# Turning the rotated heads of two units in one run of TensorE transposes, in every second unit

## The chip, the cores and the metric

The kernel runs on one core of one Trainium2 chip. The metric is the device time of one execution in microseconds (us); lower is better. The engines are called by the profile's names: PE is TensorE's matmul, PEld its weight load, DVE is VectorE, ACT ScalarE, POOL GpSimd, and SP is SyncE, which here issues nearly all DMAs.

## What is computed

The reference takes `x` (32 sequences of 32 tokens, 512 wide), adds a small per-sequence linear layer to it, and then adds an attention layer with paged keys and values:

```
x = x + einsum('bct,bcd->bdt', x, weights[subjects])
q = rope(rmsnorm(x @ Wq.T))        # 32 heads of 128
k = rope(rmsnorm(x @ Wk.T))        # 8 heads of 128
v = x @ Wv.T                       # 8 heads of 128
k_all = concat(k_cache[block_table], k)   # 512 old keys, masked by length, and 32 new ones
v_all = concat(v_cache[block_table], v)
x = x + (softmax(q k_all^T * SCALE) v_all) @ Wo.T
```

The normalised heads are rotated in halves: `t1*cos - t2*sin` and `t2*cos + t1*sin`.

## The kernel before

The kernel has two phases in one program. The first one makes queries, keys and values and writes them to DRAM. The second one computes scores, softmax, the weighted sum and the output projection for 256 pairs of a sequence and a key head. Precision is kept by splitting numbers in a high and a low half, so most products are three matmuls.

**The units of the first phase.** The 1024 tokens are 8 tiles of 128 (`g`). The columns of the weights are 12 chunks of 512 (`c`): 8 of Wq, 2 of Wk, 2 of Wv. A unit `u` is one chunk with one tile of tokens, and there are NU = 96 units in the order chunk by chunk: units 0 to 63 make queries, 64 to 79 keys, 80 to 95 values. The first NN = 80 are normalised and rotated. Each engine runs its own loop over the units, and semaphores tie the loops together.

**What becomes of a rotated unit.** PE makes 12 matmuls into one of three PSUM banks (`ps_proj`, line 1533). ACT takes the squares of the four heads (L1114). DVE multiplies the bank with the cosine and sine tables into `rot` (L1397 for queries, four instructions L1405 for keys) and signals `v_proj`. POOL adds the two products of each half into `roped`, one of NRP = 3 buffers (L909), and signals `p_sum`. Three units later (LAG = 3), PE transposes the four heads of 128x128 into one of two banks `ps_rt` (L1709) and signals `t_rt`. ACT rounds that bank to the high half in a buffer `stage` (L1127, `a_rthi`), DVE forms the low half (L1415, `v_rtlo`), and one unit later SP stores the `stage` buffer, one of NST = 8, to `q_t` or `k_new_t` in DRAM (L751). Key units also need `rstd` from POOL (L931, L933) ahead of the rotation.

**The waits around it.** In its loop PE may start unit `u` when DVE has rotated unit `u` - 3 (three banks `ps_proj`). It may transpose unit `un` when POOL has added it, and when DVE has formed the low half of unit `un` - 2, which held the same bank. POOL may write `roped` for unit `u` when unit `u` - 3 has been transposed. ACT may write `stage` for `un` when the store of `un` - 8 has landed.

**The other work in the same loops.** Each unit also carries a task on the caches and weights (`TASKS`): a 512 KB piece of a cache or of Wo is loaded into one of four buffers `c_nat` (L684), and either scanned for its largest values (ACT L1139 or DVE L1425) or converted, that is split into halves (`c_stage`, ACT L1147 and DVE L1429) and stored again (L761, L764). The load for task t + 4 is issued by SP when task t is done. The next chunk of weights is split by ACT (`wt_hi`, L1014 or L1017) and DVE (`wt_lo`, L1229 or L1233), and in the first chunk the tokens themselves are transposed and split on the way (`x0t_hi` L1021, `x0t_lo` L1223). SP also loads pages of keys into `kt`, one a unit, from unit 54 for the first sequence and from unit 80 (`NEXT_KEYS_AT`) for the second; the second one's buffer lies where the first phase's `rot` and `roped` lie.

SP takes its loop strictly in order: for unit `u` first the load of weights, then the store of turned heads, then the tasks of the unit, then pages.

Of the kernel before, what the change touches and what calls it, by code (L numbers as in the profile page):

```python
# [59 lines left out]
def build(nc, x, rows_in, table, l0_w, wq_t, wk_t, wv_t, wo_t, norms_in, kc_t, v_cache, wv,  # L60
# [186 lines left out]
    t_proj, a_proj, v_proj = sem("t_proj"), sem("a_proj"), sem("v_proj")  # L247
# [33 lines left out]
    NN = NG * (HK + NHALF)  # L281
    LAG = 3
    NCONV = 2 * NKCH

    PAGES_AT, XSUM_AT, K_TABLE_AT = 13, 15, 49
    XSUM_BOUND = float(np.sqrt(HID)) * (1.0 + 2.0**-10)
# [354 lines left out]
    def all_stored(eng):  # L641

        for i in range(NST):
            eng.wait_ge(d_st[i], 16 * (NU // NST))
        converted(eng, NCONV)

    def converted(eng, n):

        for i in range(NCS):
            eng.wait_ge(d_cst[i], 16 * len(range(i, n, NCS)))  # L650

    with persist, nc.Block() as block:
        @block.sync
        def _(sp):
# [82 lines left out]
            for u in range(NU):  # L737
                c, g = units[u]
                if u == NG:
                    sp.wait_ge(v_x0, NG)  # L740
                    sp.dma_start(x0_d.rearrange("g p h -> p g h"), x0[:]).then_inc(d_x0, 16)
                if g == 0 and c + 2 < NCK:
                    load_w(c + 2)
                if LAG < u <= NN + LAG:
                    un = u - LAG - 1
                    cn, gn = units[un]
                    kind, _, k = chunks[cn]
                    sp.wait_ge(v_rtlo, un + 1)
                    at_k = k if kind == "q" else NHALF - 1 - k
                    dst = (q_t if kind == "q" else k_new_t)[GB * gn:GB * (gn + 1), :, at_k * BLK:(at_k + 1) * BLK]  # L750
                    sp.dma_start(dst.rearrange("b d f -> d b f"), stage[un % NST][:].rearrange("p (b f) -> p b f", b=GB)  # L751
                                 ).then_inc(d_st[un % NST], 16)
                for t in TASK_IN[u]:
                    kind, n = TASKS[t]
                    if kind == "scan":
                        scanned(sp, n)
                    else:
                        what, ch = conv_kind(n)
                        sp.wait_ge(v_clo, n + 1)
                        if what == "k":  # L760
                            sp.dma_start(k_pages_t[GB * ch:GB * (ch + 1)].rearrange("a d f -> d a f"),  # L761
                                         c_stage[n % NCS][:].rearrange("p (a f) -> p a f", a=GB)).then_inc(d_cst[n % NCS], 16)
                        else:
                            sp.dma_start(v_pages[P * ch:P * (ch + 1)], c_stage[n % NCS][:]).then_inc(d_cst[n % NCS], 16)  # L764
                    if t + NCN < len(TASKS):
                        load_c(t + NCN)
                if u == NN + 3:
                    sp.wait_ge(v_scaled, 1)
                    for a in range(GB):
                        sp.dma_start(rows_d.rearrange("(q t) a c g -> a t q (c g)", t=SEQ)[a],  # L770
                                     row_part[SEQ * a:SEQ * (a + 1)].rearrange("p j c g -> p j (c g)")).then_inc(d_rows, 16)
                if u == NN + 7:
                    sp.wait_ge(d_rows, 16 * GB)
                    sp.dma_start(row_scale[:], rows_d).then_inc(d_rowl, 16)
                if u == KEYS_AT:
                    converted(sp, NKCH)
                    sp.wait_ge(v_rope, 4)
                    sp.wait_ge(v_vrow, 1)
                if KEYS_AT <= u < KEYS_AT + NPP:
                    load_pages(0, u - KEYS_AT, 1)  # L780
                if u == PREFETCH:
                    for i in range(NST):
                        sp.wait_ge(d_st[i], 16 * len(range(i, NN, NST)))
                    load_queries(0)
                    load_queries(1)
                if u == NEXT_KEYS_AT:
                    converted(sp, NCONV)
                if NEXT_KEYS_AT <= u < NEXT_KEYS_AT + NPP:
                    load_pages(1, u - NEXT_KEYS_AT, 1)
                if u in WO_LOADS:  # L790
                    wo_scanned(sp)
                    sp.wait_ge(t_rt, NN)
                    sp.wait_ge(v_wlo, HPC * (NCK - 1) if WO_LOADS[u] == 0 else HPC * NCK)
                    if WO_LOADS[u] >= 2:
                        sp.wait_ge(t_proj, NU - NG)
                    load_wo(WO_LOADS[u])
                if u == NEW_V_AT:
                    sp.wait_ge(d_st[(NU - NG) % NST], 16 * ((NU - NG) // NST + 1))
                    load_new_v(0)
                if u > NN:  # L800
                    un = u - 1
                    cn, gn = units[un]
                    sp.wait_ge(v_proj, un + 1)
                    k = HPC * chunks[cn][2]
                    sp.dma_start(v_new[GB * gn:GB * (gn + 1), :, :, k:k + HPC].rearrange("b t s j d -> (b t) s (j d)"),
                                 stage[un % NST][:].rearrange("p (s f) -> p s f", s=2)).then_inc(d_st[un % NST], 16)
            un = NU - 1
# [51 lines left out]
        def _(pool):  # L859
# [88 lines left out]

            converted(pool, NCONV)
            pool.wait_ge(v_vrow, 1)  # L950
# [50 lines left out]
        def _(act):  # L1001
# [96 lines left out]
            for u in range(NU):  # L1098
# [20 lines left out]
                else:  # L1119
                    act.wait_ge(d_st[u % NST], 16 * (u // NST))  # L1120
                    act.activation(v_staged(u, 0), ps_proj[u % NPJ][:].rearrange("p (j d) -> p j d", j=HPC),
                                   ACT.Copy, scale=scale[:, VS:VS + 1]).then_inc(a_proj, 1)
                if LAG <= u < NN + LAG:
                    un = u - LAG
                    act.wait_ge(t_rt, un + 1)
                    act.wait_ge(d_st[un % NST], 16 * (un // NST))
                    act.activation(staged(un)[:, :, 0], turned(un), ACT.Copy).then_inc(a_rthi, 1)  # L1127
# [52 lines left out]
        def _(dve):  # L1180
# [188 lines left out]
            for u in range(NU):  # L1369
# [38 lines left out]
                else:  # L1408
                    dve.scalar_tensor_tensor(v_staged(u, 1), ps_proj[u % NPJ][:].rearrange("p (j d) -> p j d", j=HPC),
                                             scale[:, VS:VS + 1], v_staged(u, 0), ALU.mult, ALU.subtract  # L1410
                                             ).then_inc(v_proj, 1)
                if LAG <= u < NN + LAG:
                    un = u - LAG
                    dve.wait_ge(a_rthi, un + 1)
                    dve.tensor_tensor(staged(un)[:, :, 1], turned(un), staged(un)[:, :, 0], ALU.subtract  # L1415
                                      ).then_inc(v_rtlo, 1)
# [113 lines left out]
        def _(pe):  # L1530
# [141 lines left out]
            for u in range(NU):  # L1672
# [25 lines left out]
                    scores(u - SCORES_AT)  # L1698
                if c == 0 and g + 2 < NG:
                    l0(g + 2)  # L1700
                if LAG <= u < NN + LAG:
                    un = u - LAG
                    pe.wait_ge(p_sum, un + 1)
                    if un == 1:
                        pe.wait_ge(v_wsum, 2)
                    if un >= 2:
                        pe.wait_ge(v_rtlo, un - 1)
                    for j in range(HPC):
                        last = pe.transpose(turned_head(un, j), roped[un % NRP][:, j, :], ident[:])  # L1709
                    last.then_inc(t_rt, 1)  # L1710
# [89 lines left out]
```

## Time and profile before

| | |
|---|---|
| median of 3 runs | 998.41 us (996.98 to 1000.1) |
| the profiled execution | 997.23 us, of which its span from first to last instruction is 995.4 us |
| first phase (PE's 96 units) | to about 346 us |
| PE busy over the span | 96% |
| DVE, ACT, POOL busy | 83%, 76%, 58% |
| TensorE's granted clock | 0.998 of full speed |

All durations used below come from the one profiled execution. Busy shares are averages over two very different phases, so they don't say which engine sets the pace in a given stretch. A matmul's duration includes its way through the array and overlaps the next one's; how fast matmuls follow each other is seen from start to start.

### The profile page before, as it was taken

The page shows a single profiled execution, that of the slowest core. Times are in us where ns is not written, and L with a number is a line of the kernel's source. Part 1 is how long each engine was busy: PE and PEld are TensorE (multiplying, and loading weights), DVE is VectorE, ACT ScalarE, POOL GpSimd, SP SyncE. Part 2 cuts the span into 40 slices and gives each one's busy share as a digit, 9 for nine tenths or more (in the row PEclk, how much of TensorE's full clock was granted, in tenths as well). Part 3 has the DMA queues.
Part 4 walks back from the last instruction along what each step waited for, and adds up shares of the span by engine and source line. Part 5 has one row for each costly group of instructions (what it writes and reads, how often), then busy time and mean ns, then how long its engine had stood idle before and what let it go on. Part 6 is the DMA issues. An engine that isn't in the chain of part 4 may idle for free.

```text
span 995.4 us, 25120 instructions
## 1 busy us (share of the span) xinstructions
PE 958.1 (96%) x8075; PEld 796.9 (80%) x8075; DVE 827.7 (83%) x1842; ACT 761.0 (76%) x2108; POOL 579.3 (58%) x861
## 2 busy tenths in 40 slices
PE   5899999999899999899999999999999999989998
PEld 4578888888677788788888888888888888878885
DVE  7889999999997689888878878888887887877880
ACT  5898999988884688878777778777777877767760
POOL 5565665565893067667755655565565656655550
PEclk9999999999999999999999999999999999999999
DMA  5899999989998899999999999999999999999940
GB/s 196 301 319 330 323 381 374 381 279 390 397 341 283 327 321 364 339 280 286 294 317 266 284 327 272 286 305 275 321 273 283 332 258 280 331 286 242 271 126 11
DMA packets 249907, 294.92 MB, mean 296 GB/s; under 512 B 79024, under 2 KB 206512, under 8 KB 247216
## 3 DMA queue, kind: packets, MB, share of 16 engines
q1 hardware_dynamic: 231088, 226.07, 76.6%
q0 software_dynamic: 18688, 67.25, 18.0%
q8 instruction: 65, 1.06, 0.4%
q14 instruction: 66, 0.54, 0.2%
HBM read 231.77 MB, written 46.27 MB: 279 GB/s over the span
## 4 chain that ended last, share of the span: by engine, by line
PE 75%; DVE 10%; POOL 5%; issue 5%; ACT 2%; DMA 2%; SPq 0%; DVEq 0%; ACTq 0%; POOLq 0%
PE ps_proj L1533 17%; PE ps_y L1533 16%; PE ps_o L1614 14%; PE ps_s L1571 8%; PE ps_t L1585 7%; PE ps_s L1575 7%; PE ps_rt L1709 2%; DMA c_nat<-in_L_cond_v_cache 2%; POOL vs L944 1%; DVE c_stage L1429 1%; DVE probs L1267 1%; DVE rot L1405 1%; PE ps_o L1626 1%; DVE stage L1415 1%; POOL probs L963 1%
## 5 line engine op out<-in xcount | busy, mean ns | idle before, releaser
L1039 ACT ACTIVATE probs<-probs,neg_max 128x544 f32<-128x544 f32 x256 | 191.6, 748 | 115.4 <-DVE neg_max L1267 100.2
L1267 DVE CUSTOM_DVE_ANT_0 probs<-ps_s,mask,row_scale 128x544 f32<-128x544 f32 x256 | 200.4, 783 | 53.7 <-PE ps_s L1575 43.3
L1614 PE MATMUL ps_o<-pt,vs 128*128 128x128 f16 x3072 | 214.0, 220 | 1.1 <-DMA vs<-v_pages,v_row 1.0
L1614 PEld LDWEIGHTS ps_o<-pt,vs 128*128 128x128 f16 x3072 | 193.1, 98 | 16.2 <-DMA vs<-v_pages,v_row 2.0
L963 POOL TENSOR_SCALAR probs<-probs,recip 128x512 f32<-128x512 f32 x144 | 99.8, 693 | 168.6 <-DVE recip L1275 164.6
L909 POOL TENSOR_TENSOR roped<-rot 128x256 f32<-128x256 f32 x160 | 144.1, 921 | 80.2 <-DVE rot L1397 76.1
L1533 PE MATMUL ps_proj<-wt_hi,x0t_hi 128*128 128x512 f32 x384 | 158.6, 414 | 6.2 <-DVE x0t_lo L1223 5.8
L1287 DVE SCALAR_TENSOR_TENSOR pt<-ps_t,pt 128x512 f16<-128x512 f32 x190 | 130.3, 686 | 35.8 <-ACT pt L1045 31.2
L1533 PE MATMUL ps_y<-wo,ot_hi 128*128 128x512 f16 x512 | 153.5, 382 | 2.6 <-DVE ot_lo L1304 2.6
L1533 PE MATMUL ps_proj<-wt_hi,x0t_lo 128*128 128x512 f32 x384 | 150.3, 393 | 0.0
L1533 PE MATMUL ps_proj<-wt_lo,x0t_hi 128*128 128x512 f32 x384 | 149.5, 391 | 0.0
L944 POOL DMA_INDIRECT vs<-v_pages,v_row x128 | 130.8, 1022 | 27.7 <-issue 10.5
L1571 PE MATMUL ps_s<-kt,qt 128*128 128x256 f16 (+1 forms) x768 | 136.3, 287 | 0.0
L1045 ACT ACTIVATE pt<-ps_t 128x512 f16<-128x512 f32 x190 | 111.9, 589 | 24.6 <-PE ps_t L1585 19.1
L1575 PE MATMUL ps_s<-kt,qt 128*128 128x288 f16 (+1 forms) x768 | 126.2, 273 | 1.5 <-DVE neg_max L1267 1.4
L1585 PE MATMUL ps_t<-fixed,probs 128*128 128x128 f32 x760 | 115.4, 275 | 5.5 <-POOL probs L963 2.4
L1585 PEld LDWEIGHTS ps_t<-fixed,probs 128*128 128x128 f32 x760 | 92.7, 141 | 32.0 <-POOL probs L957 3.8
L1114 ACT ACTIVATE squares<-ps_proj 128x128 bf16<-128x128 f32 x320 | 85.2, 296 | 22.7 <-PE ps_proj L1533 22.6
L1533 PE MATMUL ps_y<-wo,ot_lo 128*128 128x512 f16 x256 | 97.0, 379 | 0.0
L1575 PEld LDWEIGHTS ps_s<-kt,qt 128*128 128x128 f16 x768 | 73.7, 98 | 20.7 <-DVE neg_max L1267 4.2
L1533 PEld LDWEIGHTS ps_proj<-wt_hi,x0t_hi 128*128 128x128 f32 x384 | 72.2, 188 | 20.9 <-DVE x0t_lo L1223 7.1
L957 POOL TENSOR_SCALAR probs<-probs,recip 128x544 f32<-128x544 f32 (+1 forms) x64 | 43.4, 678 | 76.1 <-DVE recip L1275 74.3
(162 smaller groups left out, 1807.2 us busy)
## 6 DMA issues: line engine op xcount, KB each, us to landing
kt<-k_pages_t SPq DMA_DIRECT2D x512, 128.0 KB
c_nat<-in_L_cond_k_cache SPq DMA_DIRECT2D x32, 512.0 KB, 6.0
q_t<-stage SPq DMA_DIRECT2D x64, 256.0 KB, 6.6
c_nat<-in_L_cond_v_cache SPq DMA_DIRECT2D x32, 512.0 KB, 7.4
qt<-q_t SPq DMA_DIRECT2D x32, 512.0 KB
w_nat<-in_L_cond_Wq SPq DMA_DIRECT2D x8, 1024.0 KB, 7.7
k_pages_t<-c_stage SPq DMA_DIRECT2D x16, 512.0 KB, 5.2
c_nat<-in_L_cond_Wo SPq DMA_DIRECT2D x16, 512.0 KB, 7.1
```

The costliest lines, as they stand in the source:

```text
L909: last = pool.tensor_tensor(dst, a, b, ALU.add)
L944: pool.indirect_dma_start(vs[b % 2][:, c].rearrange("p j s d -> p (j s d)"), None, v_pages, bass.IndirectOffsetOnAxis(ap=v_row[:, b * NCH ...
L963: pool.tensor_scalar(old_keys(i), old_keys(i), col(recip, i), 1.0, ALU.mult, ALU.mult).then_inc(p_old, 1)
L1039: act.activation(pr, pr, ACT.Exp, bias=col(neg_max, i), scale=-1.0, accum_out=col(row_sum, i)).then_inc(a_exp, 1)
L1045: act.activation(pt_part(i, 0), t_bank("t", i)[:], ACT.Copy, scale=P_SCALE).then_inc(a_thi, 1)
L1267: dve.tensor_tensor_reduce(out=probs_of(i), in0=ps_s[:, score_cols(i):score_cols(i) + KEYS], in1=mask[(i // HK) % 2][:, mask_at(i):mask_at ...
L1287: dve.scalar_tensor_tensor(pt_part(i, 1), t_bank("t", i)[:], P_SCALE, pt_part(i, 0), ALU.mult, ALU.subtract).then_inc(v_tlo, 1)
L1533: ins = pe.matmul(ps, a, b, start=first and n == 0, stop=last and n == len(pairs) - 1)
L1571: pe.matmul(own[0], q[:, a], k[:, b, own[1]:own[2]], start=n2 == 0, stop=n2 == 2)
L1575: ins = pe.matmul(shared[0], q[:, a], k[:, b, shared[1]:shared[2]], start=n2 == 0, stop=n2 == 2)
L1585: ins = pe.transpose(t_bank("t", i)[:, c * P:(c + 1) * P], probs_of(i)[:, SEQ * (i % 2) + c * P:SEQ * (i % 2) + (c + 1) * P], ident[:])
L1614: ins = pe.matmul(ps_o[n % 2][:, jl * P:(jl + 1) * P], v[:, part, :], pt[pt_slot(i)][:, NCH * half + c, :], start=jl == 1 and c == 0 and k ...
```

## The change

The four transposes of a unit are no longer made in every unit. A new helper `turned_in(u)` gives, for every even `u` from 4 to 82, the two units `u` - 4 and `u` - 3, and nothing for odd `u`. PE, ACT and DVE loop over it: PE makes eight transposes, ACT two high halves, DVE two low halves. SP stores both buffers in the next, odd unit. Odd-numbered units are turned in the same iteration as before, even-numbered ones one iteration later. At unit 80 SP waits for the rotation of unit 79 (`v_proj` at NN) ahead of the page loads into the second `kt` buffer.

```diff
+    def turned_in(u):
+        return (u - LAG - 1, u - LAG) if u % 2 == 0 and LAG < u < NN + LAG else ()
...
     # SP
-                if LAG < u <= NN + LAG:
-                    un = u - LAG - 1
+                for un in turned_in(u - 1):
                     cn, gn = units[un]
                     kind, _, k = chunks[cn]
                     sp.wait_ge(v_rtlo, un + 1)
...
                 if u == NEXT_KEYS_AT:
                     converted(sp, NCONV)
+                    sp.wait_ge(v_proj, NN)
...
     # ACT
-                if LAG <= u < NN + LAG:
-                    un = u - LAG
+                for un in turned_in(u):
                     act.wait_ge(t_rt, un + 1)
                     act.wait_ge(d_st[un % NST], 16 * (un // NST))
...
     # DVE
-                if LAG <= u < NN + LAG:
-                    un = u - LAG
+                for un in turned_in(u):
                     dve.wait_ge(a_rthi, un + 1)
...
     # PE
-                if LAG <= u < NN + LAG:
-                    un = u - LAG
+                for un in turned_in(u):
                     pe.wait_ge(p_sum, un + 1)
```

## Rows read from the trace of the kernel before

**Rows 1.** The page: busy time by engine (share of the span), granted clock in slices

```profile
PE 958.1 (96%) x8075; PEld 796.9 (80%) x8075; DVE 827.7 (83%) x1842; ACT 761.0 (76%) x2108; POOL 579.3 (58%) x861
...
PEclk9999999999999999999999999999999999999999
```

**Rows 2.** Busy time in stretches: us, then busy time of each engine, clock, DMA

```profile
110.00:240.00 130.00, 129.84 (x653) 107.03 (x652) 126.48 (x148) 117.45 (x459) 79.40 (x92) 1.00 1.01 356
240.00:302.00 62.00, 56.22 (x274) 44.11 (x273) 58.25 (x101) 48.71 (x181) 54.12 (x66) 1.00 0.99 366
302.00:339.00 37.00, 37.00 (x170) 30.05 (x169) 25.82 (x49) 19.18 (x30) 5.36 (x6) 1.00 0.98 335
```

**Rows 3.** PE in order of time around one group of transposes: start, us

```profile
180.34 0.39 PE L1533 MATMUL ps_proj<-wt_hi,x0t_lo 128*128 128x512 f32 x1
180.57 0.60 PE L1709 MATMUL ps_rt<-fixed,roped 128*128 128x128 f32 x4
180.93 0.48 PE L1533 MATMUL ps_proj<-wt_hi,x0t_hi 128*128 128x512 f32 x1
181.24 0.40 PE L1533 MATMUL ps_proj<-wt_lo,x0t_hi 128*128 128x512 f32 x1
...
184.14 0.48 PE L1533 MATMUL ps_proj<-wt_hi,x0t_hi 128*128 128x512 f32 x1
```

**Rows 4.** PE in order of time: first matmuls of value units 90 and 91

```profile
327.75 0.39 PE L1533 MATMUL ps_proj<-wt_hi,x0t_hi 128*128 128x512 f32 x1
...
330.48 0.39 PE L1533 MATMUL ps_proj<-wt_hi,x0t_hi 128*128 128x512 f32 x1
```

**Rows 5.** PE in order of time, second phase: transposes in a row, f16 matmuls

```profile
353.83 0.38 PE L1594 MATMUL ps_t<-fixed,probs 128*64 128x128 f32 x2
354.05 0.49 PE L1571 MATMUL ps_s<-kt,qt 128*128 128x256 f16 x3
...
354.75 0.83 PE L1614 MATMUL ps_o<-pt,vs 128*128 128x128 f16 x12
355.42 0.50 PE L1585 MATMUL ps_y<-fixed,probs 128*128 128x128 f32 x3
```

**Rows 6.** PE, 242 to 302 us: where it stood idle, and what ended that

```profile
268.27 0.63 PE L1709 MATMUL ps_rt<-fixed,roped 128*128 128x128 f32 x4 [1.69 <-DVE stage L1415]
...
272.71 0.63 PE L1709 MATMUL ps_rt<-fixed,roped 128*128 128x128 f32 x4 [0.92 <-DVE stage L1415]
...
301.07 0.63 PE L1709 MATMUL ps_rt<-fixed,roped 128*128 128x128 f32 x4 [0.88 <-DVE stage L1415]
```

**Rows 7.** Who waited for whom, 240 to 310 us: total, times, longest

```profile
PE ps_rt L1709 <- DVE stage L1415: 5.3, 6, 1.7
...
ACT c_stage L1147 <- issue: 3.2, 2, 1.9
...
DVE rot L1405 <- ACT squares L1114: 2.1, 1, 2.1
DVE rot L1405 <- POOL rstd L933: 1.6, 2, 1.0
...
ACT c_nat L1139 <- DMA c_nat<-in_L_cond_Wo: 1.5, 3, 0.8
```

**Rows 8.** DVE in order of time, units 5 and 6

```profile
50.66 0.68 DVE L1415 TENSOR_TENSOR stage<-ps_rt,stage 128x512 f16<-128x512 f32 x1
...
56.16 0.75 DVE L1229 SCALAR_TENSOR_TENSOR wt_lo<-w_nat,w_inv,wt_hi 128x512 fp32r<-128x512 f32 x1
```

**Rows 9.** PE, start of unit 7, and its wait

```profile
53.90 0.50 PE L1533 MATMUL ps_proj<-wt_hi,x0t_hi 128*128 128x512 f32 x1 [1.29 <-DVE x0t_lo L1223]
```

**Rows 10.** DMA issues in the window 240 to 310 us: KB each, median us to landing

```profile
c_nat<-in_L_cond_v_cache SPq DMA_DIRECT2D x8, 512.0 KB, 8.1
```

**Rows 11.** Groups of instructions, 60 to 310 us: busy us, mean ns, idle before them

```profile
L909 POOL TENSOR_TENSOR roped<-rot 128x256 f32<-128x256 f32 x146 | 132.6, 929 | 76.4 <-DVE rot L1397 72.3 <-PE ps_rt L1709 2.3 <-DVE rot L1405 1.6
L1127 ACT ACTIVATE stage<-ps_rt 128x512 f16<-128x512 f32 x75 | 47.3, 631 | 1.3 <-PE ps_rt L1709 1.2
```

## Prediction

> **What bounds the kernel now.** I began with the page. PE is busy for 96% of the span at the full granted clock, and DVE for 83% [rows 1]. That says PE for the program as a whole, but the change touches only the first phase, so I cut that phase into stretches. From 110 to 240 us PE is busy for 129.8 of 130 us, with DVE close behind at 126.5 and the DMA engines at a share of 1.01. From 240 to 302 us the picture turns: PE is busy for 56.2 of 62 us and DVE for 58.3. From 302 to 339 us PE has no gap again and DVE is at 25.8 of 37 [rows 2]. So PE sets the pace for most of the phase, DVE (with ACT, POOL and the loads behind it) does for 60 us near its end, and the DMA engines are full throughout.
>
> Then I read PE in order of time. One unit with transposes goes from 180.93 to 184.14, 3.21 us [rows 3]; a value unit, which has none, from 327.75 to 330.48, 2.73 us [rows 4]. Turning four heads thus costs 0.48 us a unit, or 0.12 a head, whatever the 0.60 us duration of the group suggests. Last I listed where PE stands idle from 240 us on: six waits for DVE's low half of the bank, 5.3 us in total, 1.7 the longest [rows 6, 7].
>
> **Part 1: the transposes on PE.** Their number stays 320. What could be saved is what a group pays for being a group. From the last matmul ahead of a group to the second behind it are 0.90 us (180.34 to 181.24) [rows 3]. Without a group two steps of 2.73 / 12 = 0.2275 us stand there, 0.455 us [rows 4]. So the group costs 0.445 us by this count and 0.48 us by the whole unit. What a further transpose costs in a longer row is seen in the second phase: behind four others, two take 0.22 us until the next product, 0.11 each [rows 5]. Eight then cost 0.445 + 4 x 0.11 = 0.885 against 2 x 0.445 = 0.89 by the first count, nothing saved, and 0.92 against 0.96 by the second, 0.04 saved. For 40 pairs that is 0 to -1.6 us. I take -0.6, nearer the first count, because the rest of the unit's 0.48 can come from contention that the change doesn't remove.
>
> The gap between f32 transposes could be thought to be shorter. The Trainium skill ("TensorE: Matmul & The Clock Gate", back-to-back issue gap) gives N / 2.4 + 2.5 ns, 56 ns for 128 columns, and in the section on loading the stationary operand columns / 1.2, 107 ns. With 107 ns a head this part is worth nothing; with 56 it would be worth 8 us. The measured 0.11 agrees with the second [rows 5].
>
> **Part 2: the waits of PE.** At an even unit PE now needs the low half of unit `u` - 5 in full, ahead of the second four. It needed the same before: turning `u` - 3 waited for `u` - 5. DVE makes that low half in its own iteration `u` - 2, and the work in front of it there is the same set of instructions. At an odd unit the wait is gone. Counting the groups from the first, the longest wait (1.69 us, at 268.27) is in odd unit 71; the two others shown, and the three not shown, are in even units. But 4.4 us behind the 1.69 comes the next, at 272.71 [rows 6]: PE would arrive there earlier and wait longer for the same DVE instruction. The stall moves one unit on. It is worth something only if DVE itself is earlier, and DVE idles for 62 - 58.3 = 3.7 us there [rows 2], in three waits: 2.1 for ACT's squares, 1.6 for POOL's `rstd` [rows 7]. Behind them ACT waited 3.2 us in two pieces ahead of a conversion, with no named releaser, most likely a load [rows 7]. None of these waits for PE's transposes, so I take 0, with -3.7 us as the bound.
>
> **Part 3: the last wait.** The stretch ends at 301.07, when DVE releases the group in unit 80 [rows 6]. Before, three groups lay behind this point (77, 78, 79); now four do, since 76 is held back to make a pair. That is four transposes more, +0.4 us, and nothing later gives it back, as PE is without a gap from there on [rows 2].
>
> **Part 4: the start.** While the tokens are being split, DVE's low half at 50.66 stands ahead of the `x0t_lo` that PE waits for before unit 7 [rows 8, 9]. It moves to unit 6, so unit 7 starts up to 0.6 us earlier. But unit 8 needs the last `wt_lo` of its chunk, at 56.16 to 56.91 [rows 8], and that one has ACT's half and now two low halves in front of it, so it comes no earlier. What unit 7 gained is waited off there. I take 0, bounds -0.6 and +0.3.
>
> **Part 5: ACT, DVE, POOL.** ACT's and DVE's halves (0.63 and 0.68 us) [rows 8, 11] move from odd to even iterations. An even one gets longer and the odd one behind it shorter by as much. PE's lead of up to two units over DVE covers this; without it, each of 40 pairs would cost 0.68 us. POOL's sum of an odd unit now needs a buffer that PE frees one unit later. POOL spends 76.4 us of 250 waiting, 72.3 of it for DVE and only 2.3 for PE [rows 11]; its result is used three units later, near 9.6 us by the 3.21 us of a unit. Where DVE is late, PE has passed that point before DVE is done. I take 0; if POOL had no such time, the delay would be up to one transposed unit, 0.5 us.
>
> **Part 6: SP and the stores.** SP issues the same 80 stores, in pairs. In an odd unit `u` it waits for `u` - 5 and `u` - 4, both ready at the end of DVE's iteration `u` - 1, so no later than before; in an even unit it waits for none. Behind that wait on SP stand the next load into `c_nat`, the weights and the pages. Since SP mostly waits for DVE's conversion afterwards, two store issues fit in. A buffer of `stage` is taken again eight units after, 8 x 3.21 = 25.7 us [rows 3], against landings near 8 us [rows 10]. The new wait for unit 79's rotation at unit 80 takes the place of one for unit 76's low half, which DVE makes right behind that same rotation, so nothing in SP's queue (the 16 page loads, the stores of 76 to 79) comes later; PE first needs those pages after eight steps of the second phase. I take 0.
>
> **Sum.** -0.6 + 0 + 0.4 + 0 + 0 + 0 = -0.2 us. The profiled execution took 997.23 us, of which 995.4 are span; the forecast for it is 997.0. The median of the runs is 1.2 us above it, so the forecast for the median is 998.2 us. What a measurement of this kernel can tell from no change is about 0.3%, 3 us.
>
> **Rival 1, faster: DVE's idle time goes.** With no wait at odd units PE runs up to a transposed unit ahead, ACT's squares and POOL's `rstd` come earlier, and conversions of odd units are reached 0.68 us earlier by DVE, so their next loads start earlier. If that takes all 3.7 us of DVE's idle time out, PE ends the phase that much sooner: 998.2 - 3.7 = 994.5 us. For it: DVE has no other idle time there [rows 2, 7]. Against: those waits lead back to landings of loads, and the DMA engines are full. Chance 15%.
>
> **Rival 2, slower: the loads behind two stores.** The two stores of an odd unit, 512 KB together, are issued right before the next load into `c_nat`. DMA moves 366 GB/s there [rows 2], so the second store's 256 KB are 0.7 us of all 16 engines. The loads already take 8.1 us to land [rows 10], and a buffer must go through load, ACT, DVE and SP within four units, 4 x 3.21 = 12.8 us. ACT waited five times for such data in this window, 3.2 + 1.5 = 4.7 us in all [rows 7]. Each of them longer by 0.7 gives +3.5 us, 1001.7 us. It decides when waits at odd units grow and those at even units, whose loads have no store ahead of them, don't shrink. For it: the full DMA share. Against: the bytes are the same, and the next even unit's load gains what the odd one's loses. Chance 12%.
>
> The Trainium skill ("DMA: Bandwidth & Descriptors", queues, rings and completion order) says that each engine consumes one ring's descriptors in ring order, and SP has one ring per engine. By that a load waits out both stores, as in this rival. No run so far shows it.
>
> **Rival 3: a long row of transposes is cheaper.** If weight loads ran ahead from the fifth transpose on, they could follow each other like the f16 matmuls of the same shape, 12 in 0.67 us, 0.056 each [rows 5]. Then 160 transposes save 0.054 us each: -8.6, 989.6 us. Against it stands the 0.11 of the fifth and sixth in a row. Chance 3%.
>
> **Numbers.** The forecast has the remaining 70%, so: faster 18%, same 70%, slower 12%. Its own range, from the bounds of parts 1 to 4 other than DVE's idle time and a median that can lie 1.2 us off, is 996 to 1000 us. For 8 in 10 I reach to both nearer rivals and leave out the third: 994.2 to 1001.8 us.
>
> **What would show it.** 40 groups of eight transposes, each about 0.80 us from its first to the next product, and two units in 6.35 to 6.42 us between 110 and 240 us. No wait of PE at odd units from 242 us on, larger ones at even units, with 4 to 7 us in total. The product behind the last wait, in unit 80, 0.80 us after the transposes begin instead of the 0.36 of a group of four [rows 3]. DVE's idle time between 240 and 302 us near 3.7 us; near 0 speaks for rival 1, above 6 with longer landings for rival 2. I am wrong if the first phase's length between 110 and 240 us changes by over 1 us, or if PE waits there for anything but DVE's low half.

## The result: 3 us slower, just beyond the range

The kernel after took 1002.01 us, median of 6 runs (1000.09 to 1003.0), the kernel before 997.69 us in 6 runs beside it (996.65 to 1000.1). The ratio is 1.0031, 95% interval 1.0018 to 1.0044. A second measurement (e1 below, 11 runs against 34) gave 1000.96 against 998.11 us, 1.0029 [1.0018, 1.0041]. By their ratios both say slower by about 3 us, against a forecast of no change and a range that ended at 1001.8 us; the first median lies 0.2 us beyond that end, the second inside it.

The kernel after was profiled twice. The profiles shown here are of e1, the same kernel, because its start has no stretch of halved clock, as that of before has none; the other one starts with such a stretch, told of under the last heading. Its span is 998.5 us against 995.4. Stretches as in [rows 2], with one more, 200 to 240 us (busy time of PE, PE's weight loads, DVE, ACT and POOL; granted clock; DMA share; GB/s):

```profile
110.00:240.00 130.00, 130.00 (x656) 108.50 (x655) 124.46 (x149) 115.88 (x453) 78.37 (x93) 1.00 1.01 354
200.00:240.00 40.00, 40.00 (x201) 33.24 (x200) 38.95 (x53) 32.20 (x127) 20.72 (x24) 1.00 0.89 307
240.00:302.00 62.00, 54.69 (x260) 42.17 (x259) 55.20 (x95) 49.32 (x185) 51.80 (x63) 1.00 0.99 363
302.00:339.00 37.00, 36.08 (x167) 29.29 (x166) 26.40 (x52) 17.88 (x28) 7.87 (x10) 1.00 0.92 312
```

The same extra stretch in the kernel before:

```profile
200.00:240.00 40.00, 40.00 (x203) 33.01 (x202) 39.69 (x52) 34.62 (x137) 23.74 (x24) 1.00 0.92 319
```

PE is still without a gap until 240 us. The loss is in 240 to 302 us: PE 54.69 us busy where it was 56.22, DVE 55.20 where it was 58.25 [rows 2]. And the row that I had not read: DVE is busy for 39.69 of 40 us from 200 to 240 us in the kernel before. It had no room there, though PE was what showed as full.

PE in order of time, kernel after (e1), one group of eight transposes, then all its waits from 241 to 303 us (in brackets: idle time ahead, and what ended it):

```profile
182.79 0.40 PE L1535 MATMUL ps_proj<-wt_hi,x0t_lo 128*128 128x512 f32 x1
183.02 1.04 PE L1710 MATMUL ps_rt<-fixed,roped 128*128 128x128 f32 x8
183.81 0.47 PE L1535 MATMUL ps_proj<-wt_hi,x0t_hi 128*128 128x512 f32 x1
```

```profile
241.70 1.23 PE L1710 MATMUL ps_rt<-fixed,roped 128*128 128x128 f32 x8 [0.40 <-DVE stage L1417]
...
250.01 1.23 PE L1710 MATMUL ps_rt<-fixed,roped 128*128 128x128 f32 x8 [1.60 <-DVE stage L1417]
...
264.12 1.23 PE L1710 MATMUL ps_rt<-fixed,roped 128*128 128x128 f32 x8 [0.92 <-DVE stage L1417]
...
269.68 0.50 PE L1535 MATMUL ps_proj<-wt_hi,x0t_hi 128*128 128x512 f32 x1 [1.57 <-DVE wt_lo L1236]
...
273.14 1.23 PE L1710 MATMUL ps_rt<-fixed,roped 128*128 128x128 f32 x8 [0.44 <-DVE stage L1417]
...
291.26 0.50 PE L1535 MATMUL ps_proj<-wt_hi,x0t_hi 128*128 128x512 f32 x1 [0.81 <-DVE rot L1408]
...
295.80 1.22 PE L1710 MATMUL ps_rt<-fixed,roped 128*128 128x128 f32 x8 [1.52 <-DVE stage L1417]
```

A group takes 183.81 - 183.02 = 0.79 us. The waits ahead of transposes are now all ahead of groups of eight, so in even units; but two are new in kind, 1.57 us for `wt_lo` at the start of unit 72 and 0.81 us for DVE's rotation at unit 78. In the kernel before the list of waits from 240 to 310 us has none of PE for the rotation, and one for `wt_lo`:

```profile
PE ps_proj L1533 <- DVE wt_lo L1233: 0.3, 1, 0.3
```

The same list in e1 (total, times, longest):

```profile
DVE rot L1408 <- POOL rstd L937: 5.9, 6, 2.1
PE ps_rt L1710 <- DVE stage L1417: 5.8, 6, 1.6
POOL rstd L935 <- ACT squares L1118: 4.7, 4, 1.6
...
ACT c_stage L1150 <- issue: 4.1, 4, 2.3
...
ACT c_nat L1142 <- DMA c_nat<-in_L_cond_Wo: 2.1, 2, 1.9
...
PE ps_proj L1535 <- DVE wt_lo L1236: 1.6, 1, 1.6
```

DVE waited 5.9 us for POOL's `rstd`, where it waited 1.6 for that and 2.1 for ACT [rows 7]. Behind `rstd` stands ACT, and behind ACT, as follows, a load. Between them stands POOL itself. Its start on the key units, before and then after (e1):

```profile
263.05 0.66 POOL L931 TENSOR_SCALAR rstd<-sum_sq 128x4 f32<-128x4 f32 x1 [1.56 <-ACT squares L1114]
```

```profile
264.56 0.66 POOL L935 TENSOR_SCALAR rstd<-sum_sq 128x4 f32<-128x4 f32 x1 [1.56 <-ACT squares L1118]
```

It starts 1.51 us later, behind squares that stand behind a load issued at 254.98 instead of 253.21, and from there POOL has no gap to speak of until 283.4 us in the one kernel and 290.8 in the other. So in e1 the lateness of that load is handed on by POOL, which can't catch up; in the first profile of after POOL has gaps there, the longest 0.79 us. Durations on POOL are rough in this profile, so this is a reading of the order and not of the size.

To see where each kernel loses I use one ledger throughout: when PE starts units 24, 64 and 83, the first matmul of each unit in PE's order of time. Units 24 to 64 are PE's stretch, 64 to 83 the one in which it waits.

| profile | unit 24 | unit 64 | unit 83 | 24 to 64 | 64 to 83 |
|---|---|---|---|---|---|
| before | 109.34 | 239.31 | 307.86 | 129.97 | 68.54 |
| after | 111.44 | 240.42 | 310.96 | 128.99 | 70.54 |
| e1 (after) | 109.34 | 238.42 | 310.87 | 129.08 | 72.45 |

The change gains 0.9 to 1.0 us in PE's stretch and loses 2.0 to 3.9 us behind it, so from unit 24 to 83 it loses 1.0 and 3.0 us. About 0.4 us of the second column are four transposes that are only moved: between units 64 and 83 lie 19 groups of four before and 10 groups of eight after. The two profiles of the changed kernel reach unit 64 2.0 us apart and unit 83 0.1 us apart. PE does not decide the second date.

The chain of work that ended last says the same. By line, 200 to 225 us, before and then after (e1):

```profile
by line: PE ps_proj L1533 79.9%; PE ps_rt L1709 12.2%; DVE rot L1397 4.9%; ACT squares L1114 3.6%; PE ps_l L1723 1.2%; issue 1.2%
```

```profile
by line: DVE rot L1400 37.9%; DVE stage L1417 17.5%; issue 14.1%; DVE wt_lo L1232 11.0%; DVE c_stage L1431 10.8%; DVE abs_sums L1427 4.5%; DVE rope_k L1200 2.7%; DVE bound L1474 1.1%; DVE top_row L1250 0.8%; DVE scale L1209 0.7%; DVE bound 
```

Before, this chain runs on PE until 223 us. After, it has left PE at 194.65 us and runs on DVE. Its pieces in order of time:

```profile
194.65 1.10 issue
195.75 1.21 DVE abs_sums L1427
196.96 1.03 DVE rope_k L1199
198.00 1.15 DVE rope_k L1200
199.14 1.13 DVE rot L1400
200.27 1.20 DVE stage L1417 x2
201.47 0.87 DVE wt_lo L1232
```

DVE has, besides its usual work, the keys' rotation table (`rope_k`) and a scan there. From that point to 225 us the chain has no piece of PE, 28 us earlier than in the kernel before. That is not yet a loss: with a fifth buffer (e9 below) the chain leaves PE at the same place, at 196.14 us, and most of the loss is gone.

### The profile page after: what moved, and what is told of

Same layout as the page of the kernel before. It is cut to its first block, busy times and chain, and to the rows that moved or that the text cites. A ratio compares the mean times of both kernels' runs of the same rounds, so it can differ in the third digit from the quotient of the medians.

```text
span 999.0 us, 25120 instructions
## 1 busy us (share of the span) xinstructions
PE 960.3 (96%) x8075; PEld 799.7 (80%) x8075; DVE 826.4 (83%) x1842; ACT 762.5 (76%) x2108; POOL 577.9 (58%) x861
## 4 chain that ended last, share of the span: by engine, by line
PE 71%; DVE 11%; POOL 5%; issue 5%; DMA 4%; ACT 3%; SPq 1%; DVEq 0%; ACTq 0%; POOLq 0%
PE ps_proj L1535 16%; PE ps_y L1535 15%; PE ps_o L1616 13%; PE ps_s L1573 7%; PE ps_t L1587 7%; PE ps_s L1577 7%; PE ps_rt L1710 2%; DMA vs<-v_pages,v_row 2%; POOL vs L948 2%; DVE rot L1400 1%; DVE probs L1270 1%; DMA c_nat<-in_L_cond_v_cache 1%; DVE stage L1417 1%; PE ps_o L1628 1%; DVE rot L1408 1%
## 5 line engine op out<-in xcount | busy, mean ns | idle before, releaser
L913 POOL TENSOR_TENSOR roped<-rot 128x256 f32<-128x256 f32 x160 | 141.7, 908 | 85.0 <-DVE rot L1400 59.0
L1535 PE MATMUL ps_proj<-wt_hi,x0t_hi 128*128 128x512 f32 x384 | 155.9, 407 | 7.3 <-DVE x0t_lo L1226 5.3
```

The lines of the kernel that those rows point to most:

```text
L913: last = pool.tensor_tensor(dst, a, b, ALU.add)
L1535: ins = pe.matmul(ps, a, b, start=first and n == 0, stop=last and n == len(pairs) - 1)
```

## The experiments

All were timed beside the kernel before, so each ratio is to that kernel on the same chip. Names: "half" is a high or low half of a turned unit, "the ring" is the four buffers of `c_nat` that pass from load to ACT to DVE to SyncE and to the next load. Loads of the ring are counted from 0.

**First: where, and is it the stores?** Theory A put the loss into paired work in the key units, with rival 2 (the stores) and a chance of the clock against it.

e1: no edit. 

> The changed kernel once more, beside the three below. Theory A (the loss is real and lies in the stretch of key units, where ACT and DVE carry two halves in one iteration and PE waits for DVE): +3 us against before, PE's first matmul of unit 83 about 3 us later than before and of unit 64 under 1 us later, apart from half-clock windows. Theory B (the loss is a stretch at half clock and chance): +1 us or less.

Measured: 1.0029 [1.0018, 1.0041]. The loss is real.

e2 and e3 pair only a part of the units:

```diff
+        if u > 62:
+            return (u - LAG,) if u < NN + LAG else ()
...
```

```diff
+        if u < 63:
+            return (u - LAG,) if LAG <= u else ()
...
```

> Pairs for units 0 to 59 only; from unit 63 on every unit turns one unit as before the change. Theory A: no loss, -1 to 0 us (the transposes' own saving). If the loss comes from the start or from POOL, which waits for PE in the query units: +3 us.

Measured: 998.7 us, 1.0014 [0.9998, 1.003].

> Pairs only for units 60 to 79, single turns before. Theory A: the whole loss, +3 us, in units 64 to 82. Else: 0 to +0.5 us (the four transposes behind the last wait).

Measured: 996.79 us, 0.9995 [0.9984, 1.0007]; units 64 to 83 in 69.06 us. Theory A falls: with pairs from unit 60 on there is no loss, by the time or by the ledger (198.72 us from unit 24 to 83, against 198.52 before). PE's wait for `wt_lo` is there (1.00 us), and so is the new wait at unit 80, so neither makes the loss by itself. The loss needs paired units ahead of 60 as well.

e4 pairs only SyncE's stores:

```diff
-                for un in turned_in(u):          # PE, ACT, DVE
+                for un in turned_one(u):         # (u - LAG,)
```

> Only SP's stores are paired, in odd units; PE, ACT and DVE turn one unit in every unit as before. The theory of my rival 2 (loads into c_nat land behind two stores): +3 us, with more waits of ACT for loads between 240 and 302 us. Theory A: 0.

Measured: 997.97 us, 1.0 [0.9987, 1.0013], units 64 to 83 in 68.58 us. Rival 2 alone falls.

**Second: an interaction with the stores?** I then held that two stores back to back make SyncE issue ring loads late, and that only paired halves lack the room to take it (theory C). Rival D: the paired work alone.

e5 keeps all pairs, with one store in every unit:

```diff
-                for un in turned_in(u - 1):
+                for un in ((u - LAG - 2,) if LAG + 2 <= u < NN + LAG + 2 else ()):
```

> The kernel after with PE, ACT and DVE turning pairs in even units, but with SyncE issuing one store in every unit (the store of unit u - 5 in unit u) in place of two in every odd unit. Theory C (the loss is an interaction: two stores of 256 KB issued back to back make SyncE issue the loads into c_nat near units 58 to 63 about 2 to 3 us later, and only with paired halves is there no slack on ACT, DVE and POOL to take that up): the loss vanishes, -1 to +0.5 us against the kernel before, and the load behind ACT's conversions near 237 us is issued as early as before. Rival D (the paired work on PE, ACT, DVE and POOL alone makes the loss, stores have no part in it): +3 us, as the kernel after.

Measured: 1000.4 us, 1.0028 [1.0017, 1.004], units 64 to 83 in 71.36 us. Theory C falls with it; the stores have no measurable part.

e6 puts the loop of SyncE's tasks, with its loads, ahead of the stores. 

> The kernel after, all pairs kept, but in an odd unit SyncE issues the task's load into c_nat ahead of the two stores of rotated heads instead of behind them. Theory C: the load is no longer behind the two stores, so most of the loss goes, 0 to +1 us against before; what could remain is that the load's own wait for DVE's conversion now holds the stores back. Rival D: +3 us. If the bytes of the stores on the DMA engines, and not their place in SyncE's queue, are what counts, the loss stays at +2 to +3 too, but e5 would then be near 0.

Measured: 1003.83 us, 1.0069 [1.0051, 1.0087]. A load waits for DVE's conversion of the same unit, so the stores now stand behind that wait; that this is what costs 4 us more was not tested.

e7 and e8 move the seam to unit 48. 

> Heads turned one unit at a time for units 0 to 47, in pairs (with paired stores) for units 48 to 79. If the loss is made in the stretch of units 52 to 63 by the paired work there (theory C and D alike, since pairs from unit 60 on cost nothing): +3 to +4 us, and PE's start of unit 82 about 3 us late. If it needs a state built up over the first 48 units: 0 to +1 us.

Measured: 999.02 us, 1.0014 [1.0003, 1.0024], units 64 to 83 in 70.75 us: +2.2 in the profile, half of the expected loss in the time.

> Pairs (with paired stores) for units 0 to 47, one unit at a time for units 48 to 79. If pairs are harmless where PE sets the pace and the loss is made from unit 52 on: -0.8 to +0.3 us, the gain of 0.04 us a pair in 24 pairs or nothing of it, since DVE and the loads set the end of the stretch. If the loss comes from the early part (its loads or its state): +1.5 to +3 us.

Measured: 998.41 us, 1.0013 [1.0, 1.0026], units 64 to 83 in 67.53 us, 1.0 less than before. But a seam from pairs to single units has a price of its own: the first single unit needs the bank that DVE has only just been handed. PE waits 1.16 us there in e8 and 3.12 us in e2:

```profile
243.83 1.08 PE L1712 MATMUL ps_rt<-fixed,roped 128*128 128x128 f32 x4 [3.12 <-DVE stage L1419]
```

So e2 and e8, at 1.3 to 1.4 us, hold the price of the seam beside that of early pairs, and measure neither.

**Third: the ring.** In e5, with no paired stores, ACT stands still ahead of two conversions:

```profile
233.00 1.15 ACT L1150 ACTIVATE c_stage<-c_nat,scale 128x1024 f16<-128x1024 f32 x1 [0.66 <-issue]
...
237.31 1.15 ACT L1150 ACTIVATE c_stage<-c_nat,scale 128x1024 f16<-128x1024 f32 x1 [1.60 <-issue]
```

By their issue and landing these wait for loads 65 (issued 224.57, 8.4 us) and 66 (227.97, 9.3 us). In the kernel before load 65 landed at 231.06, ahead of its conversion at 231.60, and load 66 at 234.65, 0.13 us ahead of its own. DVE around the first conversion of V, before and then after (e1):

```profile
214.45 0.68 DVE L1415 TENSOR_TENSOR stage<-ps_rt,stage 128x512 f16<-128x512 f32 x1
215.04 1.39 DVE L1429 SCALAR_TENSOR_TENSOR c_stage<-c_nat,scale,c_stage 128x1024 f16<-128x1024 f32 x1
```

```profile
214.35 1.28 DVE L1417 TENSOR_TENSOR stage<-ps_rt,stage 128x512 f16<-128x512 f32 x2
215.55 1.48 DVE L1431 SCALAR_TENSOR_TENSOR c_stage<-c_nat,scale,c_stage 128x1024 f16<-128x1024 f32 x1
```

Two low halves (1.28 us) stand ahead of the conversion where one (0.68) stood, so it starts at 215.55 and not at 215.04, though PE is 0.5 to 0.8 us earlier there. The buffer comes free later, and so does the load into it. That is theory E; rival F has the pairs cost on DVE directly, whatever the loads do.

e9 is the kernel after, e10 the kernel before, both with

```diff
-    NCN = 4
+    NCN = 5
```

> The kernel after with five buffers of c_nat in place of four, nothing else. Theory E (the ring of c_nat is what is lost on: from unit 52 to 63 two halves stand ahead of the conversion on ACT and on DVE in even iterations, so DVE frees the buffer later, the loads numbered 65 and 66 land 1.4 to 2.1 us later against PE's place, and ACT, which works in order, waits for them ahead of the squares of units 61 and 62): with a buffer more these loads are issued a unit earlier, ACT's waits near 233 and 237 us go, and this kernel is within 1 us of e10, the kernel before with five buffers. Rival F (the pairs cost on DVE and POOL directly, through the rotation of odd units starting 0.7 us later behind two low halves, whatever the loads do): it stays 3 us above e10.

> The kernel before with five buffers of c_nat in place of four, the base for e9. If the ring also sets the end of the phase before the change (3.2 us of ACT's waiting ahead of conversions in 240 to 310 us): -1 to -3 us. If landings only get longer by as much as the loads start earlier, since the DMA engines are full: 0.

Measured: e9 998.91 us, 1.0019 [1.0009, 1.0029]; e10 997.73 us, 1.0004 [0.9993, 1.0015]. So 1.2 us are left between them by the medians and 1.5 by the ratios, against 2.9 with four buffers. In the ledger e9 takes 69.29 us for units 64 to 83 and e10 68.59, 0.7 apart against 2.0 to 3.9; from unit 24 to 83 they take 198.37 and 198.61, so nothing is lost there. What ended last, 225 to 305 us, in the kernel before, in e1 and in e9:

```profile
by line: DMA c_nat<-in_L_cond_v_cache 19.5%; DVE rot L1405 15.5%; issue 12.0%; DVE c_stage L1429 10.4%; DVE stage L1415 8.4%; PE ps_proj L1533 7.2%; DVE wt_lo L1233 7.2%; POOL rstd L933 3.9%; ACT squares L1114 3.8%; POOL roped L909 2.4%; DV
```

```profile
by line: DMA c_nat<-in_L_cond_v_cache 18.9%; POOL roped L913 13.5%; issue 13.1%; DVE rot L1408 11.2%; DVE c_stage L1431 8.8%; DVE stage L1417 7.5%; DVE wt_lo L1236 6.5%; DVE rot L1400 5.9%; POOL rstd L937 3.2%; SPq L754 2.6%; ACT squares L1
```

```profile
by line: DVE rot L1408 22.3%; DVE c_stage L1431 19.4%; DVE stage L1417 13.1%; DVE wt_lo L1236 10.1%; DVE rot L1400 8.6%; issue 6.6%; PE ps_proj L1535 6.1%; POOL roped L913 5.4%; PE ps_rt L1710 3.1%; POOL rstd L937 2.7%; DVE abs_sums L1427 1
```

The load into `c_nat` is 18.9% of that stretch in e1, and is gone from the named lines with five buffers. The chain is then mostly DVE's own work. These shares show what the chain runs through and not what it costs: in the kernel before the load has 19.5%, and there the fifth buffer gained nothing (e10). What speaks for theory E is that the fifth buffer helps the kernel with pairs alone. By e9 it takes half of the loss; e13 below, the same kernel again, puts it higher.

e11 and e12 put the second half of each pair behind the conversion or scan of its iteration, on DVE alone and on ACT and DVE:

```diff
-                for un in turned_in(u):          # ahead of the tasks
+                for un in turned_in(u)[:1]:
...
+                for un in turned_in(u)[1:]:      # behind them
```

> The kernel after, but DVE forms the second low half of a pair behind the conversion (or scan) of its iteration instead of ahead of it. Theory E: the conversion of an even iteration is 0.68 us earlier, back at its place of before, so the buffer is free earlier and a part of the loss goes: 0 to +2 us. Rival F: DVE has the same work ahead of the odd unit's rotation, +3 us. If PE then waits for the second bank at even units, more than +3.

Measured: 1004.4 us, 1.008 [1.0066, 1.0093].

> As e11, and ACT too forms the second high half of a pair behind its conversion or scan. Theory E: both orders ahead of the conversion are those of before, the loss goes except for what DVE's low half now waits for ACT: -0.5 to +1.5 us. Rival F: +3 us. Risk in both: ACT's second high half is behind a conversion that can wait for its load, then DVE and PE wait for it, and it is slower than e11.

Measured: 1002.44 us, 1.0059 [1.0042, 1.0076]. Both lose in PE's stretch, which takes 131.4 us in either against 129.1 in e1: PE now waits for the second bank. Behind it e12 needs 68.33 us for units 64 to 83, about as before the change, while e11 needs 70.47. That agrees with theory E (the conversion back at its place on both engines) but comes with another wait, so it is no clean test. Neither kernel was faster than after.

**Fourth: the remainder.** e13 repeats e9. 

> The kernel after with five buffers of c_nat once more, as the base for e14 and e15 on the same chip and for a tighter number. Theory E (a good half of the loss is the ring of c_nat): +0.5 to +2 us against the kernel before, not +3.

Measured: 999.15 us, 0.9997 [0.9982, 1.0012]; units 64 to 83 in 69.27 us, as e9. That is below the range that I had expected: by this run nothing of the loss is left. Its own median agrees with e9's (998.91); it was the kernel before that took longer here, 998.90 us against 997.34 beside e9. The intervals of e9 and e13 meet between 1.0009 and 1.0012. So the fifth buffer takes half of the loss to all of it, and rival F has what remains, if anything.

e14 is e2, and e15 pairs up to unit 75, both with five buffers. 

> Five buffers of c_nat, pairs for units 0 to 59, one unit at a time from 60 on. Theory E with a remainder that lies in the paired work from unit 60 on: the ring no longer costs, and the end of the phase comes 0 to 1 us earlier than in the kernel before, since 0.04 us a pair are gained ahead of it; time -1 to +0.5 us. Rival G (the early pairs cost by themselves, by lateness of DVE that is carried into the key units): +1 to +1.5 us, as with four buffers.

Measured: 1000.84 us, 1.0018 [1.0007, 1.0028].

> Five buffers of c_nat, pairs for units 0 to 75, units 76 to 79 turned one at a time. If the remainder of about 1 us lies behind the last waits (four transposes more behind DVE's last release, and the waits of units 79 and 81): PE's start of unit 83 is 0.4 to 1 us earlier against its start of unit 76 than in e13, time -0.4 to -1 us against e13. If it lies in units 60 to 75: no difference.

Measured: 1003.85 us, 1.005 [1.0035, 1.0066]. Both tell more of the seam than of their question. In e15 the first single units make PE wait longest of all:

```profile
302.37 0.87 PE L1712 MATMUL ps_rt<-fixed,roped 128*128 128x128 f32 x3 [3.78 <-DVE stage L1419]
```

Neither the expected gain of e15 nor that of e14 could be seen, and both stay inconclusive on whether and where something is left.

e16 turns the pairs in odd units, four buffers. 

> The kernel after with four buffers, but the pairs are turned in odd units (units 1 and 2 together, ..., 77 and 78), 0 and 79 alone. Theory E: what counts is that two halves stand ahead of every second conversion; the parity moves the delay from the loads behind even units to those behind odd ones, and the loss stays, +1.5 to +3 us. If it is only that units 60 and 61's conversions meet late loads by the accident of parity: 0 to +1 us.

Measured: 1001.89 us, 1.003 [1.0017, 1.0043]. The loss stays, as theory E expected. But this kernel has a wait of its own, 3.19 us for DVE's low half at 272.18, with a stretch at half clock beside it, and lost 1.3 us already between units 24 and 64 (131.26 us). So an equal loss doesn't show an equal cause, and the parity is not excluded.

**Fifth: what else makes the ring late.** e17 (after) and e18 (before) issue the first page loads four units later:

```diff
-    KEYS_AT, NEXT_KEYS_AT, PREFETCH, NEW_V_AT = 54, 80, 87, 93
+    KEYS_AT, NEXT_KEYS_AT, PREFETCH, NEW_V_AT = 58, 80, 87, 93
```

> The kernel after with the loads of the first batch's pages issued in units 58 to 73 in place of 54 to 69. The ring of c_nat restarts near 210 us, after the scale of V is known, and in the kernel after DVE's first conversion of V stands behind two low halves; SyncE then has two page loads, two stores of rotated heads and a store of pages ahead of the loads 65 and 66. If the ring, and what stands ahead of its loads in SyncE's queue and on the DMA engines, makes the loss: loads 65 and 66 are issued 0.5 to 1.5 us earlier against PE's place than in the kernel after, ACT's waits near 232 and 237 us shrink, and the kernel is 0 to 1.5 us above e18. If page loads have no part and only DVE's order has: 2 to 3 us above e18.

> The kernel before with the same move of the page loads, the base for e17: -1 to +0.5 us, since four buffers were not what it lost on (e10).

Measured: e17 998.59 us, 1.0017 [1.0002, 1.0033]; e18 996.9 us, 0.999 [0.9978, 1.0001]. Units 64 to 83 take 69.34 and 67.47 us. Without page loads in units 54 to 57 the kernel before is 0.9 to 1.0 us faster (its interval still holds no change), and the kernel after 1.2 (by the ratios) to 2.1 us (by the medians). Between e17 and e18 stay 1.7 us by the medians, 2.7 by the ratios and 1.9 in the ledger behind unit 64 (0.3 from unit 24 on). So the page loads seem to slow both kernels, and have at most a part in the difference, which stays without them. e18 is the best version of the study, but by 0.1%, which the runs don't tell from no change.

## Why the prediction was wrong

**The step that failed is Part 5**, "PE's lead of up to two units over DVE covers this", priced at 0. I had named what it costs without cover, 0.68 us for a pair, and then put no row beside the cover itself. The only row on it was that of 110 to 240 us, where DVE is busy for 126.5 of 130. The stretch from 200 to 240 us, with 39.69 of 40, was averaged away in it. PE looked like the only bound because it was full; DVE, full as well, was a hair behind it, and behind DVE came the ring. The chain that ended last shows it: with pairs it leaves PE at 194.65 us and does not come back until the key units. In place of Part 5's 0 stand 1.6 to 3.5 us, the 2.0 to 3.9 lost between units 64 and 83 less the 0.4 of Part 3.

**What takes the cover's place** is a sequence. Each link is seen in rows of e1; that each makes the next is inferred from the order of the engines' work: two halves ahead of an even unit's conversion (215.55 instead of 215.04); the next loads issued 0.9 and 2.4 us later in e1 (65 and 66); ACT, in order, still for 0.85 and 2.28 us ahead of conversions, with the squares of units 61 and 62 behind them; a later load, POOL 1.51 us late; `rstd` late, DVE 5.9 us idle for it; PE's waits for `wt_lo` and the rotation. That the ring carries half of the loss or more is shown by e9 and e13; that the order ahead of the conversion is what makes the ring late is read from the rows, and e11 and e12 could not show it free of another wait. That a late load alone costs nothing is shown by e4, where load 66 was issued at 230.90, 3.1 us late against PE's place, at no cost in time. So it seems that a late load costs only where the pairs have taken the room, and the pairs cost half or nothing where a fifth buffer takes the lateness. It takes both.

**Part 1** was right in its mechanism and its size: -0.6 forecast, with bounds of 0 and -1.6, and 0.9 to 1.0 us gained from unit 24 to 64, 20 pairs. PE's own idle time there before, 130 - 129.84 = 0.16 us [rows 2], went with it, which leaves 0.73 to 0.82 us, 0.04 a pair. That is the second count, not the first (0); over 40 pairs it is 1.6, the bound. A group measures 0.79 us against 0.80 forecast, two units 6.36 us, from 178.66 to 185.02 in the first profile of after, within 6.35 to 6.42. The Trainium skill ("TensorE: Matmul & The Clock Gate", loading the stationary operand), with 107 ns a head, still fits: 0.79 - 0.36 [rows 3] is 0.43 us for four further heads, 0.108 each.

**Part 2**: the waits at odd units went, those at even units grew, as said, but it took DVE's idle time from 240 to 302 us as unchanged at 3.7 us, and that grew to 6.8 (e1) and 5.6 (the first profile). It left out that the two kinds of wait that PE can have besides the bank, `wt_lo` and the rotation, could appear; they are 2.38 us in e1, and all its waits there 8.2 us, where 4 to 7 were forecast. The product behind the last wait came 0.98 us after the transposes (303.55 to 304.53), not 0.80. **Part 3**, +0.4, fits in the 0.7 us between e9 and e10 behind unit 64; no run measured it by itself, since e15 brought a wait of its own. **Part 4**: unit 24 is 80.72 us behind unit 2 in e1 and was 80.49, +0.2, inside its bound; unit 7 came 0.5 us earlier against unit 2 and unit 8 did not, as said. **Part 6**, 0, held for the stores (e4, e5). But it had SyncE's queue as harmless by the stores alone, and did not ask when DVE hands SyncE the buffer.

**The rivals.** Rival 1 went the other way: DVE's idle time grew. Rival 2 had the right sign, place (landings into `c_nat`) and size (+3.5) with the wrong cause: the stores' bytes and places cost nothing, and landings did not lengthen; the loads were issued late. The Trainium skill ("DMA: Bandwidth & Descriptors", queues, rings and completion order) has descriptors consumed in ring order; that a load then waits out the stores ahead of it was my step, and it shows in no time here (e4, e5). Rival 3 is excluded by the 0.79 us of a group.

The test that I set for being wrong, a change by over 1 us between 110 and 240 us, or a wait of PE there, did not fire (it was 0.9 to 1.0, a gain). It looked where PE is, not where DVE is.

**Open**: whether something is left with five buffers (1.2 to 1.5 us by e9, nothing by e13) and where it goes. Part 3's 0.4, the work of DVE ahead of unit 64 and the waits for `wt_lo` and the rotation are candidates that no run told apart; a part can be the clock, whose mean was 0.9967 in the runs of e9 and 0.9974 in those of e10. Open too is whether the order of two halves and conversion alone starts the sequence, as e11, e12 and e16 each brought a wait of their own, and what POOL has of it.

## What to carry to other kernels

Batching two small steps on the engine that is full also batches their companions on engines that are nearly full. Cut the profile until each stretch has one regime, and ask of each engine above 95% in it what stands behind the delayed instruction, down to the buffer that it frees. In a ring of buffers with a load of 8 us, half a microsecond ahead of the release can be paid by an in-order engine that waits for that load; here it was paid only where the engines behind it were full. A share in the chain that ended last is not a price: try the cure on the kernel before too, as e10 did. When an experiment changes the grouping in mid-loop, look for the wait that the seam itself makes.

## What the runs showed of the hardware

**The granted clock can fall at a wait of PE, in the middle of the kernel too.** At the end of a wait of 3.12 us in e2 (row above), the clock was 0.51 of full from 243.7 to 247.1 us, half of 2.4 GHz:

```profile
243.70:247.10 3.40, 3.27 (x10) 2.82 (x11) 2.88 (x4) 2.47 (x9) 2.10 (x4) 0.51 1.04 400
```

After 2.24 us idle (e11, at 271.48) and 3.19 us (e16, at 272.18) it was halved for 3.4 us as well, after 2.57 us (e14, at 245.42) from 246.8 on, and after 3.78 us (e15) for 6.8 us. In e11, e15 and e16 the fall came 0.4 to 1.4 us ahead of the end of the wait. A wait of 2.53 us (e6, at 252.12) was followed by none, and neither were the waits up to 1.81 us in after and e1 from 240 to 303 us. At the start of the program PE waits 2.83 us ahead of unit 2 in both kernels, and the half clock follows it in some executions and not in others: after has it from 29.7 to 33.1 us, before and e1 don't. Each such stretch there costs 1.6 us (unit 3 at 34.94 against 32.95 in e1, less the 0.4 by which unit 2 was later). Times of one kernel go with its mean clock. Among the runs of e1, those with a clock of 0.998 took 999.35 us in the mean for the kernel after (3 runs) and 997.31 for the one before (12); at 0.996 it was 1001.20 (4) and 998.16 (11). So at an equal clock 2 to 3 us of loss remain: it is not the clock's. Its mean over all of them was 0.9963 after and 0.9969 before.

**An issue on SyncE's queue has no fixed price.** Issuing one store of pages to `v_pages` took 0.33 us at 217.06, when nothing had been issued for 4.8 us, and 2.14 us at 226.55, behind six other issues in 3.7 us (e1). In the kernel before the second one took 1.15 us, at 225.18. Why it takes longer no run tells. The rows of e1:

```profile
217.06 0.33 SPq L767 DMA_DIRECT2D v_pages<-c_stage  x1
```

```profile
225.48 1.03 SPq L754 DMA_DIRECT2D q_t<-stage  x2
226.55 2.14 SPq L767 DMA_DIRECT2D v_pages<-c_stage  x1
228.73 0.67 SPq L688 DMA_DIRECT2D c_nat<-in_L_cond_v_cache  x1
```

The load into `c_nat` behind it waits for that in turn. Landings, counted from the issue, did not lengthen, while the loads still came late: from 240 to 310 us the median is 7.2 us in e1 and 7.3 in the first profile of after, shown here, against 8.1 before [rows 10].

```profile
c_nat<-in_L_cond_v_cache SPq DMA_DIRECT2D x9, 512.0 KB, 7.3
```
